# Placing the feed-forward items one step denser in the attention loop of an eight-core transformer layer

## The reference, cut to what matters

```python
scores = jnp.einsum('bhqd,bhkd->bhqk', q, k) * hs ** (-0.5)
p = jax.nn.softplus(scores); p = p * p; p = p * causal
attn = p / (jnp.sum(p, axis=-1, keepdims=True) + 1e-09)
x = _layernorm(x + attn_out @ w_proj.T + b_proj)
probs = softmax(x @ router_w.T); topk_vals, topk_idx = top_k(probs, 2)
out = ((expert_out[topk_idx] + probs[topk_idx]) * weights).sum()
x = _layernorm(x + out)
```

## Time and profile before

| | us |
|---|---|
| median of 2 runs | 2053.76 (2017.24 and 2090.28) |
| the profiled execution | 2025.0 |
| span of its slowest core (core 6) | 2023.3 |
| spans of the eight cores | 1993.3 to 2023.3 |
| busy: PE / ACT / DVE / POOL | 1458.3 / 1234.7 / 1156.0 / 245.7 |

### The profile page before, as it was taken

How to read it: one execution, slowest core, us unless ns; L and a number is a source line. 1 busy time by engine, 2 the same in 40 slices (tenths; PEclk the granted TensorE clock), 3 DMA queues, 4 the chain that set the end, 5 groups by cost and what they waited for, 6 DMA issues and landing times.

```text
span 2023.3 us, 25963 instructions; the slowest of 8 cores (1993.3 to 2023.3 us)
## 1 busy us (share of the span) xinstructions
PE 1458.3 (72%) x7836; PEld 645.0 (32%) x7968; DVE 1156.0 (57%) x1524; ACT 1234.7 (61%) x687; POOL 245.7 (12%) x362
## 2 busy tenths in 40 slices
PE   1868756767777776576887877988878436699991
PEld 0333323333333232242332423433323112344440
DVE  0016757667776666565655656656666647444447
ACT  0228858888887967989779678797799810000000
POOL 1011101111111001020120110201101001022110
PEclk9877778888789988799999989999999758699995
DMA  9877687867877025064371462824301024054542
GB/s 158 114 114 124 89 181 113 128 104 116 132 113 116 1 42 79 0 88 75 56 115 24 80 93 43 116 47 71 56 11 22 0 89 119 7 83 68 79 63 83
DMA packets 146384, 162.47 MB, mean 80 GB/s; under 512 B 8784, under 2 KB 135888, under 8 KB 146128
## 3 DMA queue, kind: packets, MB, share of 16 engines
q0 software_dynamic: 137328, 128.10, 44.3%
q1 hardware_dynamic: 8928, 32.71, 4.6%
HBM read 269.65 MB, written 16.97 MB: 142 GB/s over the span
## 4 chain that ended last, share of the span: by engine, by line
PE 33%; ACT 29%; DMA 15%; DVE 11%; issue 10%; POOL 1%; DVEq 1%; ACTq 0%; SPq 0%; POOLq 0%
ACT spb L1066 14%; ACT t_exp L1066 14%; PE psK L1066 12%; PE psV L1066 12%; PE psS L1066 4%; DMA xkb<-xkf 4%; DMA scr<-rsb 3%; DVE pbb L1066 3%; DMA bcb<-scr 3%; PE psA L1066 2%; PE psB L1066 2%; DMA xq<-xqf 2%; DVE rsb L1066 2%; DMA qall<-ew 2%; DVE stream L1066 2%
## 5 line engine op out<-in xcount | busy, mean ns | idle before, releaser
L1066 ACT ACTIVATE t_exp<-psS 128x2048 bf16<-128x2048 f32 x320 | 600.7, 1877 | 210.5 <-PE psS L1066 187.1
L1066 ACT ACTIVATE spb<-t_exp 128x2048 bf16<-128x2048 bf16 x320 | 611.3, 1910 | 80.1 <-DVE pbb L1066 38.1
L1066 DVE TENSOR_TENSOR pbb<-spb 128x2048 bf16<-128x2048 bf16 x320 | 390.3, 1220 | 262.2 <-ACT spb L1066 234.8
L1066 PE MATMUL psS<-qall,kb 64*128 64x512 bf16 x1280 | 214.7, 414 | 210.8 <-ACT t_exp L1066 184.0
L1066 PE MATMUL psA<-pbb,vb 128*65 128x512 bf16 x640 | 274.2, 428 | 70.4 <-DVE vb L1066 32.7
L1066 PE MATMUL psB<-pbb,vb 128*65 128x512 bf16 x640 | 271.4, 424 | 0.0
L1066 ACT ACTIVATE lnr<-lnv 128x4 f32<-128x4 f32 (+1 forms) x6 | 1.2, 206 | 362.4 <-DVE lnv L1066 362.4
L1066 DVE TENSOR_TENSOR pbb<-pbb,mkb 128x2048 bf16<-128x2048 bf16 x128 | 156.8, 1225 | 13.4 <-DVE pbb L1066 0.2
L1066 DVE SCALAR_TENSOR_TENSOR stream<-psK,gates,stream 128x512 f32<-128x512 f32 x128 | 95.6, 747 | 119.0 <-PE psK L1066 118.3
L1066 PEld LDWEIGHTS psA<-pbb,vb 128*65 128x65 bf16 x640 | 75.0, 117 | 270.8 <-issue 241.7
L1066 DVE SCALAR_TENSOR_TENSOR stream<-psV,gates,stream 128x512 f32<-128x512 f32 x128 | 96.0, 750 | 111.1 <-PE psV L1066 110.7
(11 more groups left out here) (90 smaller groups left out, 1394.0 us busy)
## 6 DMA issues: line engine op xcount, KB each, us to landing
xkb<-xkf POOLq DMA_DIRECT2D x64, 1024.0 KB, 12.1
qall<-ew POOLq DMA_DIRECT2D x64, 256.0 KB, 7.1
ewh<-ew POOLq DMA_DIRECT2D x64, 256.0 KB, 5.7
wqK<-wq POOLq DMA_DIRECT2D x16, 512.0 KB, 8.7
stream<-xot SPq DMA_DIRECT2D x16, 512.0 KB, 11.0
wqA<-wq POOLq DMA_DIRECT2D x8, 768.0 KB, 23.8
out<-stream SPq DMA_DIRECT2D x12, 512.0 KB, 2.6
kvs<-vb SPq DMA_DIRECT2D x8, 520.0 KB, 10.9
```

The costliest lines, as they stand in the source:

```text
L1066: instr = getattr(eng, method)(*args, **kw)
```

## The change

Two constants of the rules are lowered. `heavy_done` is set from the start only in the last step of a pass (3.15), no more in the last two (3.14 and 3.15). `v_cool` is set to 1 after a tag-2 item, no more to 2; since it is lowered at the head of the next step before it is looked at, the next step may take a tag-2 item. (In passes 0 to 7 the queue is empty.) No instruction is added or removed; their places in the engines' orders change.

```diff
-                    if slot == PASS_SLOTS[p][1] and j >= npair - 2:
+                    if slot == PASS_SLOTS[p][1] and j >= npair - 1:
                         heavy_done = 1
                     if epi_q:
                         epi_q.pop(0)()
@@
                         if tag:
                             heavy_done = 1
                         if tag == 2:
-                            v_cool[0] = 2
+                            v_cool[0] = 1
```

## The result

| | before | after |
|---|---|---|
| median, us | 2025.18 (10 runs) | 2043.09 (11 runs) |
| ratio after to before | | 1.009 (1.0073 to 1.0108) |
| profiled execution, us | 2025.0 | 2044.1 |
| spans of the eight cores | 1993.3 to 2023.3 | 2003.6 to 2042.3 |

The changed kernel is 18 us slower, 0.9%. With more runs the median of before is 2025.18; the 2053.76 of the first two runs had one disturbed run in it. The forecast was 2044.1.

The account below looks back on a forecast made before the run. ScalarE was taken to set the loop step at 4.03 us, TensorE in steps 2.1 to 2.10 with K/V groups. Terms 17.0 - 6.6 + 11.7 - 3.0 = +19.1 on 2025.0 gave 2044.1 us, range 2022 to 2068.

Parts of the forecast that it names:

- Where the items go: Queue 4 items ahead in pass 10, rising to 9 in pass 15; last expert item moves from 3.2 to 2.5.
- The last pass, +17.0: Pass 15: ln2 items packed back to back on VectorE lose 22.2 us instead of 5.2; bounds 10 and 22.
- The freed steps 3.14: Step 3.14 of a pass: an expert item there fits under ScalarE's 4.03 us step and costs nothing.
- Behind the loop, -6.6: After the loop: about 9.2 us of VectorE work gone, TensorE gains 6.6 us; between -4 and -9.2.
- R3: Rival: lower TensorE clock removes the gain behind the loop and slows matmuls after load waits; time 2062, chance 0.19.
- Weight loads, +11.7: Passes 10 to 14: TensorE's new waits for expert weights, less old ones of 13.2 us; from 0 to +22.
- Pass 9, -3: Pass 9: ln1 batch without a multiply ahead gains 5 us, filled empty steps cost 2; from -6 to +3.
- Sum: Whole kernel: four terms add to +19.1 us on the profiled 2025.0, giving 2044.1.
- Chances: Whole kernel: within 2% of before 0.87, slower by more 0.11, faster by more 0.02.
- R2: Rival: packed VectorE work hides under ScalarE, so the kernel is faster or equal; 2015 without load waits, chance 0.07.
- R1: Rival: weight loads do not bind, new and old waits even out, +11.7 becomes 0; time 2032, chance 0.17.
- R4: Rival: the change does nothing, counts differ but waits stay; time 2025, chance 0.05.

Follow-up runs that it names:

- third run above: The changed kernel with the ten ln2 items placed exactly as before the change, everything else as changed: ratio 1.0033 to before.
- one site: The changed kernel with the x loads emitted behind the fourth weight load, only in step 2.11 of pass 13: one time of 2033.15 us.
- the early loads above: All four weight loads of a half emitted at item 1 of the half before, not items 4 to 7: 1.0014 on the changed kernel, 0.9976 on the kernel before.

## Why the prediction was right or wrong, point by point

**Where the items go.** As counted, with one slip: the half end of pass 14 that I moved to 2.7 stays at 2.8.

**The last pass, +17.0.** Measured +15.4. Exp 3.3 came 56.8 us behind exp 2.6 on the slowest core (1539.54 to 1596.34), forecast 58.5. Undoing it alone returned it (third run above). The cycle of two stats was 0.7 over a step, not 0.9, as the run with the items in 3.2 to 3.11 shows (0.87 and 0.86 less 0.14). The freed steps 3.14 cost nothing, as forecast.

**Behind the loop, -6.6.** Measured -4.4. From the first residual add to the ln1 batch of the second rows the distance fell from 51.4 to 46.5 (medians), 4.9; but the first add came 1.6 later behind the last exp (42.3 for 40.7). It waited for the residual loads, which left at 28.3 for 28.1 and had all landed at 42.2 for 40.6; why they took longer is not shown. Granted clock on the slowest core, last steps of the loop and first projections (windows; us, PE, PEld, DVE, ACT, POOL, PEclk, DMA share, GB/s):

```profile
1592.00:1646.00 54.00, 28.24 (x96) 7.47 (x96) 20.04 (x22) 46.86 (x27) 0.00 (x0) 0.67 0.00 1
...
1670.00:1700.00 30.00, 18.26 (x53) 5.69 (x53) 12.31 (x18) 0.00 (x0) 0.62 (x2) 0.67 0.67 249
```

R3's direction is there: 0.67 in the last twelve steps for 0.76 before. The first three groups of eight projection matmuls took 3.57 us each and the next 1.89, the two levels of the clock. How much of the missing 2.2 us this is was not tried; it did not change the order of terms.

**Weight loads, +11.7.** The new waits were, on the profiled core, pass 10: 9.23 for 7.8; pass 13: 6.35 for 5.0 and 6.58 for 9.2; and pass 12: 7.07 where I had 2.9. Together 29.2 for 24.9. The last is the mis-sized one: I took the mean of the two shorter waits instead of working out which loads stand behind the x load of 2.5, as I had done for 2.3. In the passes that holds +8.2, -6.3, -4.3, +17.0 and -1.1 for 10 to 14, +13.5 in sum. The place is shown as the cause at one site (134.2 for 143.9) and, less exactly, for all.

**Pass 9, -3.** Measured -7.5; this is the term that was most mis-sized. Its two parts came as forecast: the steps round the batch, 2.5 to 2.8, gave 4.6 (5 forecast), and the others in which items moved cost 1.8 (1.1 in 2.0 and 2.1, 0.7 in 2.9 to 2.11; 2 forecast). The sum had no term for ln1_stats(6), which moved from the step of the second reciprocal to that of the first: 2.2 to 2.4 fell from 19.8 to 15.5, the one step behind it from 11.17 to 4.92, while 2.3 grew by 2.5. TensorE's projection behind it, before and after:

```profile
748.21 3.19 PE L1066 MATMUL psK<-wpT,attn 128*128 128x512 bf16 x7 [4.75 <-DVE vb L1066]
...
743.47 1.89 PE L1066 MATMUL psK<-wpT,attn 128*128 128x512 bf16 x8 [1.68 <-DVE vb L1066]
```

It waited for the copies that empty psK and psV, which stood behind the reciprocal and the stats item in VectorE's order, and in the kernel before it then ran at the lower level of the clock (seven recorded matmuls in 3.19 us, eight in 1.89 after).

**Pass 14, step 2.9.** It fell from 8.49 to 5.35 although the items stand in the same steps, and the trace says how: before, the scratch stores among the weight loads took up to 11.9 us to land (8.9 after), the broadcast was held until then, and its multiply waited 2.73 us (0.27 after). It is the chain of the early loads above, and it was there before the change.

**Sum.** Forecast 17.0 - 6.6 + 11.7 - 3.0 = 19.1; measured 15.4 - 4.4 + 13.5 - 7.5 + 1.0 (pass 8, not forecast) = 18.0. The misses of 1.6, 2.2, 1.8, 4.5 and 1.0 have both signs; that the sum comes this close is partly luck.

**Chances.** Here the prediction failed. The step is "2% of 2025 is 40 us, about what a measurement of this kernel can tell from no change": it put 0.87 on no difference beyond that, and so let its own +0.9% pass for no difference. The runs tell far less than 2%: the interval is 0.35% wide over all, and 0.9% lies clear of 1. With terms of +17 and +12 against -7 and -3, each seen in rows, "slower, by about one per cent" was what the sum said, and the chance should have been on that side. Also, R2's time of 2015 lay outside the stated range of 2022 to 2068, though it had a chance of 0.07.

**Rivals.** R1 (loads do not bind) falls by the waits of 29.2. R2 falls: time lost in a step is not regained in the empty ones. The last twelve steps were 4.02 to 4.30 us each. R4 falls by the ratio.

## What to carry to other kernels

A filler item is not free by its own size but by what stands in the same step on its engine: the ten ln2 items cost 11.8 us back to back and 20.5 back to back under masks, copies and broadcasts, while four of the stats spaced out cost 0.4, and three in the idle time behind the loop did not move the last attention multiply (27.5 with and without). Moving a list forward moves every later item into another neighbour and its loads to another place in the queue, so work out both for each item, not only the number of steps saved. Issue a load as soon as its buffer is free, ahead of the large ones, but look at what then stands behind it on the queue: the early weight loads took 27.5 us out of the places that had waited and put 9.0 back where they held up small stores.

## What the runs showed that I had not expected

- Small transfers suffer from large ones of another queue: broadcast to multiply 7.15 us with four 512 KB loads issued 1 us earlier on SyncE's queue, 3.4 without, 3.1 before; scratch stores of 2 KB 5.8 to 6.3 us to land with eight such loads in flight, 1.6 without. Order on one's own queue does not protect.
- 29 us of TensorE waiting for weights were worth 27.5 us of exp distance where they stood, and 15 in the time of the kernel, because the cure slowed other transfers.
- VectorE's order sets TensorE's waits in the K/V steps: a reciprocal of 1.7 us and a stats item ahead of the copies that empty both background banks made TensorE wait 4.75 us; with the same stats item one step earlier it waited 1.68, and the three steps together were 4.3 us shorter.
